# Attention stage of a gated cross-attention and MoE kernel: values projected for four pairs of heads, reciprocals from two activations and one Newton step, row norms two at a time, routing steps at other places, and the products with the values right behind the scores

## The chip, the cores and the metric

One core of a Trainium2 chip runs the whole program. The metric is the device time of one execution in microseconds (us). Only one core runs, so there is no other core to wait for.

## What is computed

The reference, cut to what matters (batch 8, 512 rows of x, 1024 rows of context, width 256, 16 heads of 64):

```python
lat, ctx = layer_norm(layernorm(x)), layer_norm(context)
q = lat @ Wq                       # 16 heads of 64
k, v = split(ctx @ Wkv)            # 16 heads of 64 each
k = apply_rope(k, cos, sin)        # cos and sin by token
attn = clip(q @ k.T * 64 ** -0.5, -11, 11)
out = softmax(attn) @ v
x = x + tanh(g_xattn) * (out @ Wo + bo)
# then, on layernorm(x): 64 experts, the best 8 of each row out of the
# best 4 of 8 groups (sigmoid scores plus a correction bias), and a shared expert
x = x + tanh(g_ffn) * (routed + shared)
```

## The kernel before

The program has four blocks in a row: `setup` (splits the weights into a high and a low part, so that TensorE multiplies them with the precision of fp32 in three passes), `attention`, `finish_routing`, `experts`. The change is in `attention` and in a few lines of `setup`.

**Pairs and steps.** `attention` works on 8 batches of 8 pairs of heads. A pair g goes through eight steps, c = 0 to 7. In step c of pair g TensorE does, in the order of the code of `step` for `pe`:

- the scores of token tile c of the *previous* pair (L897, six matmuls of 512 columns, written to the PSUM tile `scores`),
- where there is one, a tile of value projections (L913, `ps_v`), a half of the keys (L928, `ps_k`, in c = 0 and 4) or the queries (L940, `ps_k`, in c = 2) of the pair g itself,
- the products of values with exponentials (L952, written to `ps_o`) of the tile that was scored two steps earlier; the tile of the last two steps is done in c = 0 and 1 of the next pair, where also the sum of the exponentials over tokens is formed (L960, `ps_y`, c = 1),
- a half of the output projection (L989, `ps_y`) in c = 4 and 6.

A tile's exponentials go from ScalarE (L1029, `e`) to GpSimd, which clips them (L1124), and from there both to TensorE (L952) and to VectorE, which adds them up (L1297, `e_sum`). ScalarE also copies `ps_o` to `o_raw` in c = 2 (L1024); the product of tile 0 in c = 2 writes `ps_o` again and so waits for that copy (`s_oraw`). VectorE takes the reciprocals of the sums straight from `ps_y` in two halves of 256 columns (L1265, c = 2 and 3), and GpSimd multiplies `o_raw` with them (L1120, L1127).

Keys are turned by the rotary tables: ScalarE swaps quarters of `ps_k` into `k_sw` (L1043), VectorE multiplies with cosine and sine (L1281, L1282), GpSimd adds (L1116), ScalarE keeps the high part (L1051) and VectorE the low part (L1287). The low part of the queries is L1276 (`q_t`, semaphore `s_qlo`), for which the second half of the keys (c = 4) waits, since it writes `ps_k` again.

**Values.** `ps_v` holds 256 columns, two pairs of heads at once ("doubles"). Eight tiles of tokens make 32 groups of six matmuls in a batch. In batch 0 and in the first pair of every batch they stand in all eight steps of the even pairs; else four of them stand in each pair (`value_tile`). The last pair has none.

**Between batches** `boundary` turns the normalised rows `x_nat` of the next batch (L876, 24 transposes), which wait for the last normalised row tile (`norms.normed`) and for the last exponentials. Rows are normalised one tile of 128 rows at a time during the pairs (`prepare`): statistics on VectorE (L77, L82), the inverse root on GpSimd (L102; two operations for a context tile, seven for a latent tile), then L90 on VectorE. The last of them stands in c = 7 of the last pair.

**Routing.** From batch 1 on, the rows of the batch before are routed to experts between these steps (`route`, on VectorE, with short work of TensorE and ScalarE), and GpSimd sends the rows of the batch before that out by indirect DMA (L1105), one in each of the steps 0, 1, 4, 5, 7 of the pairs p = 1 to 6. Batches 2 to 7 are one loop body.

Every engine runs its own list in the order written; only semaphores connect them.

## Time and profile before

| | us |
|---|---|
| median of 3 runs | 2636.36 (2633.79 to 2646.41) |
| profiled execution, time | 2636.81 |
| profiled execution, span | 2634.7 |

| engine | busy us | share of the span |
|---|---|---|
| TensorE | 2331.4 | 88% |
| VectorE | 2171.2 | 82% |
| GpSimd | 1789.0 | 68% |
| ScalarE | 1420.3 | 54% |

TensorE runs at 2.4 GHz nearly everywhere (mean granted clock 0.959). These are averages over the whole program. What a change in the attention stage is worth is read from that stage: from the windows of single pairs, and from what TensorE waited for in them.

### The profile page before, as it was taken

The numbers are of one execution on the slowest core, as the hardware profiler recorded it, in microseconds if no ns is written. First come the engines' busy times: TensorE is split into PE (matmuls) and PEld (weight loads), VectorE is DVE, ScalarE is ACT, GpSimd is POOL, SyncE is SP. The second block draws the span as 40 slices with busy tenths as digits, with TensorE's granted clock in tenths as the row PEclk, the third lists the DMA queues.
The fourth block names the chain that finished last, engine by engine and source line by source line (L and its number), as shares of the span: only waits on it lengthen the run. The fifth ranks groups of instructions, "written<-read, shape, count | busy, mean of one in ns | idle before, by whom it ended". The sixth has DMA issues, their size and how long they took to land. (4 is left out here: it accounts for less than half of the span.)

```text
span 2634.7 us, 43493 instructions
## 1 busy us (share of the span) xinstructions
PE 2331.4 (88%) x12227; PEld 1360.2 (52%) x12227; DVE 2171.2 (82%) x3638; ACT 1420.3 (54%) x2520; POOL 1789.0 (68%) x1723
## 2 busy tenths in 40 slices
PE   2999999899989998998999899989987968999980
PEld 2554545454444544454545445444543646987870
DVE  4888788898888898898888898988897676688884
ACT  3666556565555555555665556555552323666660
POOL 3777676488858876886787588758874730077776
PEclk9999999899999999999999899999997988999995
DMA  8434334011102111120111112111114408799994
GB/s 298 155 124 159 112 112 162 29 58 55 63 29 78 57 51 44 57 69 31 65 53 54 40 57 77 53 42 55 56 49 147 157 16 291 235 329 322 332 322 138
DMA packets 166488, 305.11 MB, mean 116 GB/s; under 512 B 20914, under 2 KB 100210, under 8 KB 166002
## 3 DMA queue, kind: packets, MB, share of 16 engines
q1 hardware_dynamic: 138162, 234.88, 26.2%
q0 software_dynamic: 24576, 67.14, 7.7%
q8 instruction: 114, 1.87, 0.3%
q14 instruction: 116, 0.95, 0.1%
q10 hardware_dynamic: 3520, 0.27, 0.1%
HBM read 172.46 MB, written 129.76 MB: 115 GB/s over the span
## 5 line engine op out<-in xcount | busy, mean ns | idle before, releaser
L1124 POOL TENSOR_SCALAR e<-e 128x1024 f32<-128x1024 f32 x520 | 639.8, 1230 | 406.1 <-ACT e L1029 379.5
L1029 ACT ACTIVATE e<-scores 128x1024 f32<-128x1024 f32 x520 | 533.4, 1026 | 530.5 <-PE scores L897 509.0
L1297 DVE TENSOR_TENSOR e_sum<-e_sum,e 128x1024 f32<-128x1024 f32 x391 | 585.9, 1498 | 47.5 <-POOL e L1124 44.9
L952 PE MATMUL ps_o<-e,v 128*64 128x512 f32 x2088 | 567.7, 622 | 1.6 <-POOL e L1124 1.6
L897 PE MATMUL scores<-q_t,k_t 64*128 64x512 f32 x3120 | 505.3, 429 | 15.5 <-DVE affine L1242 14.2
L897 PEld LDWEIGHTS scores<-q_t,k_t 64*128 64x128 f32 x3120 | 255.0, 186 | 377.1 <-issue 255.4
L1831 POOL DMA_INDIRECT more<-results_in_blocks,index x256 | 245.4, 959 | 210.2 <-DMA results_in_blocks<-more 129.6
L1043 ACT ACTIVATE k_sw<-ps_k 32x512 f32<-32x512 f32 x512 | 301.3, 588 | 114.6 <-PE ps_k L928 110.0
L1105 POOL DMA_INDIRECT rows_in_blocks<-room,a_r_index_now x192 | 247.9, 1291 | 50.9 <-issue 50.1
L913 PE MATMUL ps_v<-wv,ctx_t 128*128 128x256 f32 x1536 | 252.5, 301 | 0.0
L928 PE MATMUL ps_k<-ctx_t,wqk 128*128 128x512 f32 x768 | 218.6, 422 | 33.8 <-DVE q_t L1276 33.5
L913 PEld LDWEIGHTS ps_v<-wv,ctx_t 128*128 128x128 f32 x1536 | 199.8, 190 | 94.2 <-issue 93.9
L1265 DVE RECIPROCAL r_den<-ps_y 128x256 f32<-128x256 f32 x132 | 230.4, 1746 | 13.6 <-PE ps_y L960 12.6
L1768 PE MATMUL ps_out<-down_all,room 128*128 (+1 forms) x640 | 194.5, 386 | 4.3 <-DVE room L1810 3.4
L928 PEld LDWEIGHTS ps_k<-ctx_t,wqk 128*128 128x128 f32 x768 | 140.3, 196 | 98.1 <-DVE q_t L1276 49.4
L1287 DVE TENSOR_TENSOR k_t<-k_c,k_t 128x512 fp32r<-128x512 f32 x128 | 118.5, 926 | 81.0 <-ACT k_t L1051 81.0
L952 PEld LDWEIGHTS ps_o<-e,v 128*64 128x64 f32 x2088 | 104.2, 136 | 143.1 <-issue 103.4
L1116 POOL TENSOR_TENSOR k_c<-k_c,k_sw 128x512 f32<-128x512 f32 x128 | 173.5, 1355 | 3.0 <-DVE k_sw L1282 1.3
L1793 DVE SCALAR_TENSOR_TENSOR x<-more,gate,x 128x256 f32<-128x256 f32 x256 | 123.2, 481 | 53.9 <-DMA more<-results_in_blocks,index 52.7
L1775 PE MATMUL ps_x<-ident,x_nat 128*128 128x128 f32 x640 | 125.5, 279 | 44.3 <-PEq L1312 27.6
L1731 ACT ACTIVATE x_nat<-ps_x 128x256 f32<-128x256 f32 x320 | 121.0, 378 | 78.2 <-PE ps_x L1775 75.0
L1748 PE MATMUL ps_hid<-x_nat,room 128*128 128x128 f32 x1024 | 157.7, 277 | 2.3 <-DVE room L1806 1.4
(287 smaller groups left out, 3606.3 us busy)
## 6 DMA issues: line engine op xcount, KB each, us to landing
rows_in_blocks<-room SPq DMA_DIRECT2D x16, 2560.0 KB, 9.8
x_nat<-rows_in_blocks SPq DMA_DIRECT2D x160, 256.0 KB
results_in_blocks<-more SPq DMA_DIRECT2D x80, 512.0 KB
wqk<-wqk_pairs SPq DMA_DIRECT2D x65, 512.0 KB, 3.5
wv<-wv_doubles SPq DMA_DIRECT2D x33, 512.0 KB, 3.3
wo<-in_L_xattn_Wo SPq DMA_DIRECT2D x66, 128.0 KB, 3.4
x_nat<-in_ctx SPq DMA_DIRECT2D x64, 128.0 KB, 3.2
down_all<-in_L_ffn_down_w SPq DMA_DIRECT2D x16, 512.0 KB, 8.6
```

What stands on the lines that cost most here:

```text
L897: mm = pe.matmul(scores[:, c % 2, hh * N:(hh + 1) * N], k_t[rows, att, kp, c * P:(c + 1) * P], q_t[rows, att, qp, :], start=(part == 0), s ...
L913: mm = pe.matmul(ps_v[:, 0:2 * P], ctx_t[:, a, cc, tile * P:(tile + 1) * P], wv[:, bb, cc], start=(k == 0), stop=(k == 5))
L928: mm = pe.matmul(ps_k[:], wqk[:, jj, bb, cc, 1], ctx_t[:, a, cc, half * N:(half + 1) * N], start=(k == 0), stop=(k == 5))
L952: mm = pe.matmul(ps_o[hh * DH:(hh + 1) * DH, :], v[:, tile, buf, hh * DH:(hh + 1) * DH], e[:, tile % 4, hh * N:(hh + 1) * N], start=(tile ...
L1029: act.activation(e[:, c % 4], scores[:, c % 2], ACT.Exp, scale=SCALE).then_inc(s_exp, 1)
L1043: st = act.activation(k_sw[to], ps_k[of], ACT.Copy)
L1105: pool.indirect_dma_start(xs_dram, bass.IndirectOffsetOnAxis(ap=router.index_now[:, t, k:k + 1], axis=0), router.rows[:, t], None).then_in ...
L1124: pool.tensor_scalar(e[:, c % 4], e[:, c % 4], EXP_HI, EXP_LO, ALU.min, ALU.max).then_inc(s_clip, 1)
L1265: dve.reciprocal(r_den[:, half], y_flat[:, half]).then_inc(s_rec, 1)
L1297: dve.tensor_tensor(total, e[:, 0] if c == 2 else total, e[:, tile % 4], ALU.add).then_inc(s_sum, 1)
L1768: pe.matmul(ps_y[:, i % 4, 0:D], act_g[:, i % 4], w, start=True, stop=True).then_inc(s_dn, 1)
L1831: pool.indirect_dma_start(land[:, k], None, y_dram[0:(E_R + (b + 1) * BODY) * P, :], bass.IndirectOffsetOnAxis(ap=at, axis=0)).then_inc(y_ ...
```

## The change

1. **Values of four pairs.** `DOUBLES` becomes `QUADS`: `ps_v` is used with 512 columns, `v` holds four pairs instead of three, and a batch has 16 groups of six matmuls. They stand in the first two of every four pairs (m = 0: c = 3, 5, 6, 7; m = 1: c = 1, 3, 5, 7), none in m = 2 and 3.
2. **Reciprocals.** In c = 2 ScalarE takes `Ln` and then `Exp` with scale -1 of the sums; in c = 3 VectorE makes one Newton step of it (a product of 512 columns, then one instruction over two SBUF tiles). The sign is put right by `minus_gate`. GpSimd's first half of `o_n` moves behind the clip of c = 3. Table sets are loaded by hand: `Tanh` of the router needs another one and back, once in a batch.
3. **Norms.** From batch 1 on two row tiles are normalised together, in the pairs 1 to 6 (statistics in c = 0, roots in c = 1, results in c = 6), and the context of a batch is loaded in one DMA.
4. **Routing steps** move: `number_blocks`, `place` and `cross` from the last pair to the first pair of the next batch, the steps of the groups to earlier places, and `e_sum` has one buffer instead of two. The first copies of rows go out one step later.
5. **Order.** The products of values with exponentials stand right behind the scores, ahead of the projections.

The core of the diff:

```diff
+                if attend or c < 2:
+                    tile = (c + 6) % 8
+                    buf = (m + 3 if c >= 2 else m + 2) % 4
+                    pe.wait_ge(s_clip, 1 + g * 8 + c)
+                    if c == 2:
+                        pe.wait_ge(s_oraw, g + 1)
+                    if m == 2 and c == 1:
+                        pe.wait_ge(s_v, 1 + (g // 4 + 1) * 8)
+                    for hh in range(2):
+                        mm = pe.matmul(ps_o[...], v[:, tile, buf, ...], e[:, tile % 4, ...], ...)
+                    mm.then_inc(s_pv, 1)
+
                 if first and c in (0, 4):
                     pe.wait_ge(t_lo, 1 + b * 6 + (2 if c == 0 else 4))
...
-                            mm = pe.matmul(ps_v[:, 0:2 * P], ctx_t[:, a, cc, tile * P:(tile + 1) * P], wv[:, bb, cc],
+                            mm = pe.matmul(ps_v[:], ctx_t[:, a, cc, tile * P:(tile + 1) * P], wv[:, bb, cc],
                                            start=(k == 0), stop=(k == 5))
...
-                if attend or c < 2:
-                    tile = (c + 6) % 8
-                    buf = values_of(m + 3 if c >= 2 else m + 2)
-                    pe.wait_ge(s_clip, 1 + g * 8 + c)
...
+                if c == 2:
+                    act.wait_ge(s_den, 1 + g + 1)
+                    act.activation(r_den[:], y_flat, ACT.Ln).then_inc(s_log, 1)
+                    act.wait_ge(s_log, g + 1)
+                    act.activation(r_den[:], r_den[:], ACT.Exp, scale=-1.0).then_inc(s_seed, 1)
...
-                if c in (2, 3):
-                    half = slice((c - 2) * D, (c - 1) * D)
-                    dve.wait_ge(s_den, 1 + g + 1)
-                    dve.reciprocal(r_den[:, half], y_flat[:, half]).then_inc(s_rec, 1)
...
+                if c == 3:
+                    dve.wait_ge(s_seed, g + 1)
+                    dve.tensor_tensor(o_n[:], y_flat, r_den[:], ALU.mult).then_inc(s_part, 1)
+                    dve.wait_ge(s_part, g + 1)
+                    dve.scalar_tensor_tensor(out=r_den[:], in0=o_n[:], scalar=2.0, in1=r_den[:],
+                                             op0=ALU.subtract, op1=ALU.mult).then_inc(s_rec, 1)
```

TensorE, steps 2 to 4 of pair 2 of the loop body, before (L897 scores, L940 queries, L952 products with the values, L913 values, L928 keys):

```order
L897 MATMUL scores<-q_t,k_t 128x512 [waits s_exp]
L897 MATMUL scores<-q_t,k_t 128x512 x5
L940 MATMUL ps_k<-lat_t,wqk 128x512 [waits s_cos]
L940 MATMUL ps_k<-lat_t,wqk 128x512 x5
L952 MATMUL ps_o<-e,v 64x512 [waits s_oraw,s_clip]
L952 MATMUL ps_o<-e,v 64x512
...
L928 MATMUL ps_k<-ctx_t,wqk 128x512 [waits s_cos,s_qlo]
L928 MATMUL ps_k<-ctx_t,wqk 128x512 x5
L952 MATMUL ps_o<-e,v 64x512 [waits s_clip]
L952 MATMUL ps_o<-e,v 64x512
```

The same place after (L908 scores, L921 products with the values, L964 queries, L952 keys):

```order
L908 MATMUL scores<-q_t,k_t 128x512 [waits s_exp]
L908 MATMUL scores<-q_t,k_t 128x512 x5
L921 MATMUL ps_o<-e,v 64x512 [waits s_oraw,s_clip]
L921 MATMUL ps_o<-e,v 64x512
L964 MATMUL ps_k<-lat_t,wqk 128x512 [waits s_cos]
L964 MATMUL ps_k<-lat_t,wqk 128x512 x5
...
L921 MATMUL ps_o<-e,v 64x512 [waits s_clip]
L921 MATMUL ps_o<-e,v 64x512
L952 MATMUL ps_k<-ctx_t,wqk 128x512 [waits s_cos,s_qlo]
L952 MATMUL ps_k<-ctx_t,wqk 128x512 x5
```

The product of tile 0, which waits for `o_raw`, has passed ahead of the queries, and the product of tile 2 ahead of the second half of the keys; the value tile that stood between them is gone from this pair.

VectorE, between the sine product of c = 1 and the sum of c = 3, pair 3 of the loop body, before:

```order
L1282 TENSOR_TENSOR k_sw<-k_sw,sin_t 128x512
...
L1265 RECIPROCAL r_den<-ps_y 128x256 [waits s_den]
...
L1297 TENSOR_TENSOR e_sum<-e 128x1024 [waits s_den,s_clip]
L1265 RECIPROCAL r_den<-ps_y 128x256 [waits s_den]
L1276 TENSOR_TENSOR q_t<-ps_k,q_t 128x512 [waits s_qe]
```

After:

```order
L1321 TENSOR_TENSOR k_sw<-k_sw,sin_t 128x512
...
L1336 TENSOR_TENSOR e_sum<-e 128x1024 [waits s_den]
L1308 TENSOR_TENSOR q_t<-ps_k,q_t 128x512 [waits s_qe]
L1311 TENSOR_TENSOR o_n<-ps_y,r_den 128x512 [waits s_seed]
L1313 SCALAR_TENSOR_TENSOR r_den<-o_n,r_den 128x512 [waits s_part]
```

The two reciprocals ahead of the low part of the queries (`q_t`) are gone, and two instructions stand behind it.

## Rows read from the trace of the kernel before

**Rows 1.** The page, part 1: engine, busy us, share of the span, count.

```profile
PE 2331.4 (88%) x12227; PEld 1360.2 (52%) x12227; DVE 2171.2 (82%) x3638; ACT 1420.3 (54%) x2520; POOL 1789.0 (68%) x1723
```

**Rows 2.** Windows: length, busy of PE, PEld, DVE, ACT, POOL, clock.

```profile
65.21:250.84 185.63, 185.63 (x952) 94.29 (x950) 157.46 (x167) 113.40 (x171) 138.81 (x126) 1.00 0.42 141
997.72:1240.01 242.29, 225.03 (x1136) 117.32 (x1137) 213.06 (x293) 138.51 (x208) 185.69 (x174) 0.98 0.16 54
1212.59:1240.01 27.42, 17.81 (x86) 7.70 (x83) 26.52 (x38) 11.35 (x15) 16.08 (x14) 0.97 0.06 19
1240.01:1255.62 15.61, 13.82 (x62) 9.91 (x64) 9.12 (x16) 10.91 (x18) 1.84 (x2) 0.72 0.14 51
```

**Rows 3.** Waits of PE from 60 to 1990 us: us in total, times, longest.

```profile
PE scores L876 <- DVE x_nat L90: 42.5, 7, 6.6
PE ps_k L928 <- DVE q_t L1276: 33.5, 20, 3.1
PE ps_y L313 <- DVE x L1272: 13.7, 7, 2.1
PE ps_y L437 <- DVE x L1272: 9.4, 7, 1.4
```

**Rows 4.** Groups by line: count, busy us, mean ns, idle before.

```profile
L1265 DVE RECIPROCAL r_den<-ps_y 128x256 f32<-128x256 f32 x132 | 230.4, 1746 | 13.6 <-PE ps_y L960 12.6
L1281 DVE TENSOR_TENSOR k_c<-ps_k,cos_t 128x512 f32<-128x512 f32 x128 | 87.7, 685 | 29.9 <-ACT k_sw L1043 29.1
L1287 DVE TENSOR_TENSOR k_t<-k_c,k_t 128x512 fp32r<-128x512 f32 x128 | 118.5, 926 | 81.0 <-ACT k_t L1051 81.0
```

**Rows 5.** Timeline of PE, start and length in us, steps 0 to 2 of a pair.

```profile
1063.46 1.65 PE L928 MATMUL ps_k<-ctx_t,wqk 128*128 128x512 f32 x6
1065.04 1.08 PE L952 MATMUL ps_o<-e,v 128*64 128x512 f32 x4
1066.05 0.96 PE L897 MATMUL scores<-q_t,k_t 64*128 64x512 f32 x6
1066.94 0.98 PE L913 MATMUL ps_v<-wv,ctx_t 128*128 128x256 f32 x6
1067.85 1.08 PE L952 MATMUL ps_o<-e,v 128*64 128x512 f32 x4
1068.76 1.03 PE L960 MATMUL ps_y<-e_sum,ones_dh 128*64 128x512 f32 x4
1069.72 0.97 PE L897 MATMUL scores<-q_t,k_t 64*128 64x512 f32 x6
...
1078.75 1.08 PE L952 MATMUL ps_o<-e,v 128*64 128x512 f32 x4
```

**Rows 6.** Timeline of ACT at the same steps.

```profile
1065.15 2.39 ACT L1043 ACTIVATE k_sw<-ps_k 32x512 f32<-32x512 f32 x4 [0.47 <-PE ps_k L928]
1067.56 1.02 ACT L1029 ACTIVATE e<-scores 128x1024 f32<-128x1024 f32 x1
...
1069.06 0.60 ACT L1024 ACTIVATE o_raw<-ps_o 128x512 f32<-128x512 f32 x1 [0.19 <-PE ps_o L952]
```

**Rows 7.** Timeline of POOL from step 1 of the same pair on.

```profile
1068.79 1.03 POOL L1124 TENSOR_SCALAR e<-e 128x1024 f32<-128x1024 f32 x1 [0.72 <-ACT e L1029]
...
1076.25 1.04 POOL L1124 TENSOR_SCALAR e<-e 128x1024 f32<-128x1024 f32 x1
...
1077.65 1.88 POOL L297 TENSOR_TENSOR a_r_rstd<-a_r_rstd,minus_half 128x4 f32<-128x4 f32 x1
...
1085.47 1.03 POOL L1124 TENSOR_SCALAR e<-e 128x1024 f32<-128x1024 f32 x1
...
1091.64 1.04 POOL L1124 TENSOR_SCALAR e<-e 128x1024 f32<-128x1024 f32 x1
```

**Rows 8.** Timeline of PE at the boundary in front of batch 2.

```profile
511.86 4.31 PE L876 MATMUL scores<-ident,x_nat 128*128 128x128 f32 x24 [5.49 <-DVE x_nat L90]
518.71 1.65 PE L897 MATMUL scores<-q_t,k_t 64*128 64x512 f32 x6 [2.54 <-DVE affine L1242]
```

More of the change, by code:

```diff
@@ L15 @@
 PAIRS = H // 2
[L16 removed]
+QUADS = PAIRS // 4
 NT = N // P
@@ L629, in _ @@
             act.wait_ge(wq_loaded, 16 * 4)
-            for n in range(3 * DOUBLES):
+            for n in range(5 * QUADS):
                 for c in range(C2):
@@ L670, in _ @@
         def _(dve):
-            for n in range(3 * DOUBLES):
+            for n in range(5 * QUADS):
                 dve.wait_ge(w_hi, C2 * (n + 1))
@@ L1097, in prepare @@
                                       n_step + (1 - jj) * norms.LAT_STEPS)
-            places = [(0, 7)] + [(p, c) for p in range(1, 7) for c in (0, 1, 4, 5, 7)] + [(7, 0)]
+            places = [(p, c) for p in range(1, 7) for c in (0, 1, 4, 5, 7)] + [(7, 0), (7, 1)]
             places.sort()
@@ L1167, in finish_slots @@
                 if part == 0:
-                    router.r, router.k = r, crossing[0]
+                    router.r, router.k = r, numbered[0]
+                    router.number_blocks(dve, range(3, 6))
+                elif part == 1:
+                    router.place(dve)
+                    router.cross(dve)
+                elif part == 2:
                     router.slots(dve)
-                elif part == 1:
+                elif part == 3:
                     router.order_slots(dve)
```

210 lines of the change are left out of this document (115 added, 95 removed).

## The prediction

> **What bounds the kernel now.** The page comes first: TensorE is busy for 88% of the span and VectorE for 82% [rows 1]. That is an average, so I went to windows inside the attention stage. In batch 0 TensorE is busy for all 185.63 us of the window, with VectorE at 85%, so nothing but TensorE's own work sets the time there. A later batch lasts 242.29 us, of which TensorE works 225.03. The missing 17 us lie at few places: the last pair (27.42 us with 17.81 of work) and the boundary behind it (15.61 us, at a granted clock of 0.72) [rows 2]. The waits of TensorE name the reasons, all of them VectorE: the last normalised row tile, 42.5 us in 7 boundaries; the low part of the queries in front of the second half of the keys, 33.5 us; and the rows `x` that VectorE adds up late, 13.7 and 9.4 us, in front of router work [rows 3]. In short, TensorE's work is the bound, with VectorE late at the end of each batch. The other rows show what a step costs (rows 5) and what ScalarE and GpSimd do meanwhile (rows 6, 7).
>
> **What the change takes away, per batch of 1 to 7.**
>
> Values. A group of six matmuls of 256 columns costs 0.91 us from start to start (1066.94 to 1067.85), six of 512 columns for the keys cost 1.58 (1063.46 to 1065.04) [rows 5]. 32 x 0.91 = 29.1 becomes 16 x 1.58 = 25.3: -3.8, and -3.5 since some of the old groups stand in front of keys or queries and cost a little less there. Bound above: 512 columns cost twice 0.91, nothing gained. I take the keys' row, which is the same shape.
>
> The boundary. The last norm goes to pair 6, and about 7 us of VectorE's work leave the last pair. The 42.5 / 7 = 6.1 us wait [rows 3] goes; what is late next is the exponential of tile 7 (1.02 us [rows 6], with a product of 1.01 to cover it), 0.25 us. That is -5.8. Behind it the first score started 6.85 us after the first transpose [rows 8], and the product of sums 15.61 us after it in the window at clock 0.72 [rows 2]. Without the long idle time before it I expect 6.4 and then, at full clock, 0.89 + 1.01 + 1.58 + 0.89 + 0.91 = 5.3, together 11.7. Of the 3.9 us between, 1.6 are two value groups that only move: -2.3.
>
> The low part of the queries. VectorE's two reciprocals of 1746 ns [rows 4] stood in front of it and are gone. The wait was 33.5 / 7 = 4.8: -4.8. In place of 3.5 us a pair VectorE has two instructions of 512 columns: the first reads PSUM and SBUF, as `k_c` does (685 ns), the second two SBUF tiles, as `k_t` (926 ns) [rows 4], together 1.6. They stand behind the queries' low part, so only the output product in c = 4 waits for them.
>
> Router waits. 13.7 + 9.4 us in 7 batches = 3.3 [rows 3], both from a late VectorE: -3.3, at worst half of it.
>
> Together -3.5 - 5.8 - 2.3 - 4.8 - 3.3 = **-19.7 us**.
>
> **What it adds.** This comes mostly from the new order, since TensorE executes its list in order and now meets each product before the projection that used to cover its wait.
>
> `o_raw` in c = 2. After the keys' matmuls start, ScalarE runs `k_sw` (start +1.69, 2.39 us), an exponential (+4.10, the next start 0.92 later) and the copy of `o_raw` (0.60): ready at +5.67 [rows 6]. TensorE reaches the product after 1.58 + 0.89 + 0.91 + 0.96 + 0.89 = 5.24 [rows 5]. Before, 1.6 us of queries stood between; now it waits 0.43. In pair m = 1 a value group is in between and hides it: 6 of 8 pairs, +2.6. Bounds 0 and 6 x 0.8.
>
> The clip of tile 2, in front of the product in c = 4. GpSimd starts the clip of tile 1 at 1068.79 and that of tile 2 at 1076.25, 7.46 us later: in between stand a row transfer, seven root operations and the sum of the keys. With two root operations (c = 5 and 6 of the pair) the same stretch takes 6.17, from 1085.47 to 1091.64 [rows 7]. TensorE's product waited for nothing at 1078.75, because queries, a value group and the keys covered it [rows 5]. In a pair without value groups (p = 2, 3, 6, 7) TensorE now wants it 1.90 + 5.24 + 0.43 + 1.01 + 1.59 + 0.89 + 1.01 + 0.89 = 12.96 us after the pair begins, and tile 1's clip starts at 1.90 + 4.10 + 1.02 = 7.02. In pair 2 (seven operations) the clip is ready at 7.02 + 7.46 + 1.04 = 15.52: +2.5. In pairs 3 and 6 (two) at 14.23: +1.25 each. Pair 7 has none, and pairs 0, 1, 4, 5 have a value group, 1.58, in front. Sum +5.0. Bounds: 2 if GpSimd is quicker because VectorE disturbs it less, 10 if it is late from pair to pair.
>
> The first output product in c = 4. In pair 2 GpSimd also has the router's root (1.88 us [rows 7]) ahead of it: +1.65. In pairs 0 and 5 the moved routing steps (some 5 and 3 us of VectorE in c = 1 and 2) push the Newton step: +0.7 and +0.8. Sum +3.2, bounds 1 and 6.
>
> The rest (products in c = 0, the sums' product in c = 1 when VectorE is behind after pair 0): +1.0, bounds 0 and 3. Together **+11.8**. The new `Ln` and `Exp`, 0.6 us each as `o_raw` [rows 6], lie in ScalarE's idle time, and their chain behind the queries' copy (0.6 + 0.6 + 0.6 + 1.6) ends before GpSimd gets to `o_n`; without that cover they would add about 1 us a pair. ScalarE works 138.51 of 242.29 us [rows 2].
>
> Net per batch -7.9, times 7 = **-55.3**. Batch 0 had no wait to lose: values -1.6 (12 of its old groups stood in front of keys or queries), `o_raw` +2.6, the clip of tile 2 twice 1.1 (no row transfers yet): **+3.2**. A third more of `v` is cleared at the start, +1, for which I have no row. The one big context load replaces eight small ones at a DMA share of 0.16 [rows 2] and is needed two pairs later: nothing. Sum -51. The profiled execution took 2636.8 us and the median of the runs is 2636.4, so both give 2586.
>
> **Two rules of the skill that speak against it.** The row shows one thing for VectorE: 512 elements cost 685 ns with one operand in PSUM and 926 ns with both in SBUF [rows 4]. The Trainium skill (SBUF — State Buffer, "SBUF: two separate sides") says that a VectorE instruction with two SBUF inputs locks GpSimd's reads out for its whole length. The old reciprocal read PSUM only, so by that rule the second Newton instruction is new trouble for GpSimd; it is rival 3 below. The profile's rows show `Exp` and `Copy` in steady alternation with no gap for tables [rows 6]. The Trainium skill (ScalarE: Activation LUTs, "What ACT_TABLE_LOAD costs") gives 2.66 us for a switch of table sets; two in each of seven batches would be 37 us of ScalarE by that page, an estimate, and 2623 if TensorE waited for all of it. ScalarE's idle time says it does not.
>
> **Rivals.**
> 1. *The waits fall together.* One wait of TensorE lets ScalarE and GpSimd catch up, so that `o_raw`, clip and output product are paid once. Half of 11.8: -13.8 a batch, 2544. For it: no product waited for a clip in before's batches. Against it: `o_raw` comes first in the pair and delays its own chain.
> 2. *Values at twice the old price*: +3.5 x 8, 2614. Against it stands the keys' row.
> 3. *GpSimd held up by the second Newton instruction*: 0.93 in six pairs a batch, 5.6: net -2.3 x 7, batch 0 +7: 2629.
> 4. *Slower: GpSimd late in every pair.* The order takes the cover from all pairs, not from three. If all four pairs without values lose pair 2's 4.6 us and the others 1.6, that is 24.8 + 1 against 19.7: +6.1 x 7 + 8 + 1, 2689. It decides from 2.7 us of new waits a pair; I count 1.5. For it: GpSimd works 185.69 of 242.29 us, and a pair without values is only 23 us of TensorE, in which GpSimd needs 23 to 25 by its rows. Against it: fewer root operations (22 instead of 44 a batch).
>
> **How the numbers follow.** Forecast 0.50 at 2586 (its own range 2560 to 2612); rival 1 0.21; rival 2 0.06; rival 3 0.14; rival 4 0.09. From 2540 to 2640 leaves out some of rival 1 and all of rival 4. A measurement of this kernel can tell about 0.5% from no change, 2623 to 2650. Faster: forecast, rivals 1 and 2, a little of 3: 0.77. Within: most of 3: 0.14. Slower: 0.09.
>
> **What would show it.** Right: no wait of `scores` for `x_nat`, none or little of `ps_k` for `q_t`; new rows of waits of `ps_o` for `o_raw` (about 20 us in all) and for clips of `e` (about 40), of `ps_y` for `o_n` (20); a value group of 1.58; batches of about 235 us, with the gain at the boundary and a loss in pairs 2, 3 and 6. Wrong: waits for clips also in pairs with values, or GpSimd busy over 90% in the window of a batch (rival 4); no new wait above 5 us (rival 1); clip durations longer behind the Newton step (rival 3).

## The result, and the profile after

| | before, us | after, us |
|---|---|---|
| median | 2638.38 (4 runs) | 2661.60 (2659.68 to 2663.80, 4 runs) |
| profiled execution, span | 2634.7 | 2657.9 |
| start of the last product of sums (`ps_y`, end of the attention stage) | 1999.2 | 2021.7 |
| length of batch 0 | 223.7 | 231.5 |
| length of batches 1 to 6, mean | 243.0 | 244.3 |
| start of the first batch | 49.7 | 51.0 |
| last batch, to its product of sums | 267.7 | 273.5 |

The ratio is 1.0083 [1.0059, 1.0106]: **slower** by 0.8%, which is clear of the noise, where 2586 us (2540 to 2640) had been forecast. Of the difference of 23 us, 22.5 stand before the last product of sums; what follows it takes some 636 us in both. Batches are taken here from the first transpose to the next batch's, and the last one ends with that product of sums. Before's row of the page is in [rows 1]; this is after's (engine, busy us, share, count):

```profile
PE 2310.5 (87%) x11459; PEld 1286.0 (48%) x11459; DVE 2116.3 (80%) x3593; ACT 1498.1 (56%) x2536; POOL 1804.5 (68%) x1569
```

TensorE and VectorE have less to do, and the program takes longer. The windows that answer to [rows 2] follow: the stretch in batch 0, batch 4, its last pair, the boundary behind it up to the product of sums, and pair 2 of batch 4 (length, busy PE, PEld, DVE, ACT, POOL, clock).

```profile
65.21:250.84 185.63, 178.20 (x822) 84.63 (x820) 137.54 (x160) 114.53 (x162) 135.30 (x122) 1.00 0.41 141
1010.77:1256.54 245.77, 223.62 (x1040) 108.77 (x1041) 207.12 (x288) 147.86 (x211) 186.66 (x153) 0.97 0.16 53
1235.27:1256.54 21.27, 18.01 (x84) 7.79 (x85) 20.43 (x24) 12.65 (x18) 15.12 (x12) 1.00 0.09 34
1256.54:1272.01 15.47, 10.76 (x50) 6.29 (x52) 10.57 (x14) 8.78 (x14) 3.38 (x3) 0.78 0.05 15
1087.60:1119.68 32.08, 26.37 (x116) 12.05 (x112) 27.04 (x41) 18.15 (x27) 27.37 (x27) 0.89 0.17 60
```

In the stretch of batch 0 TensorE was busy for all 185.63 us before and is busy for 178.20 now: it has room that the other engines don't fill. The last pair is 6.1 us shorter (27.42 before), the boundary only 0.1 us (15.61). All other pairs together are 9.8 us longer. TensorE's waits, as in [rows 3], from 60 to 1990 us:

```profile
PE ps_o L921 <- POOL e L1147: 56.2, 31, 3.7
PE ps_y L1001 <- POOL o_n L1151: 22.9, 24, 3.0
PE scores L887 <- DVE affine L1278: 18.5, 6, 3.3
PE ps_o L921 <- ACT o_raw L1038: 18.5, 35, 1.4
PE scores L908 <- ACT affine L1020: 12.4, 7, 2.3
PE ps_y L973 <- DVE e_sum L1336: 10.0, 7, 1.5
PE ps_k L952 <- DVE q_t L1308: 9.1, 6, 1.5
PE scores L887 <- DVE x_nat L90: 4.5, 1, 4.5
```

The waits of [rows 3] for `x_nat` (42.5), `q_t` (33.5) and `x` are gone or small. In their place stand waits for clips and `o_n` of GpSimd, for `o_raw`, and at the boundary for `affine`. Three groups that answer to [rows 4] and [rows 5] (count, busy us, mean ns): the values and the two instructions of the Newton step.

```profile
L937 PE MATMUL ps_v<-wv,ctx_t 128*128 128x512 f32 x768 | 212.1, 411 | 0.0
L1313 DVE SCALAR_TENSOR_TENSOR r_den<-o_n,r_den 128x512 f32<-128x512 f32 x64 | 50.4, 788 | 2.2
L1311 DVE TENSOR_TENSOR o_n<-ps_y,r_den 128x512 f32<-128x512 f32 x64 | 44.0, 687 | 16.9 <-ACT r_den L1064 16.9
```

### The profile page after: what moved, and what is told of

It is laid out like the page before. It is cut to its first block and busy times, and to the rows that moved or that the text cites. A ratio compares the mean times of both kernels' runs of the same rounds, so it can differ in the third digit from the quotient of the medians.

```text
span 2657.9 us, 41338 instructions
## 1 busy us (share of the span) xinstructions
PE 2310.5 (87%) x11459; PEld 1286.0 (48%) x11459; DVE 2116.3 (80%) x3593; ACT 1498.1 (56%) x2536; POOL 1804.5 (68%) x1569
## 5 line engine op out<-in xcount | busy, mean ns | idle before, releaser
L1147 POOL TENSOR_SCALAR e<-e 128x1024 f32<-128x1024 f32 x520 | 673.8, 1296 | 405.0 <-ACT e L1043 345.8
L1336 DVE TENSOR_TENSOR e_sum<-e_sum,e 128x1024 f32<-128x1024 f32 x391 | 628.9, 1608 | 92.0 <-POOL e L1147 86.9
L921 PE MATMUL ps_o<-e,v 128*64 128x512 f32 x2088 | 575.4, 629 | 76.9 <-POOL e L1147 57.3
L908 PE MATMUL scores<-q_t,k_t 64*128 64x512 f32 x3120 | 507.8, 430 | 14.2 <-ACT affine L1020 12.4
L908 PEld LDWEIGHTS scores<-q_t,k_t 64*128 64x128 f32 x3120 | 255.9, 187 | 276.8 <-issue 246.9
L1132 POOL DMA_INDIRECT rows_in_blocks<-room,a_r_index_now x192 | 272.2, 1418 | 49.0 <-issue 44.2
L921 PEld LDWEIGHTS ps_o<-e,v 128*64 128x64 f32 x2088 | 105.8, 136 | 275.4 <-issue 162.6
L952 PE MATMUL ps_k<-ctx_t,wqk 128*128 128x512 f32 x768 | 220.1, 423 | 9.1 <-DVE q_t L1308 9.1
L937 PE MATMUL ps_v<-wv,ctx_t 128*128 128x512 f32 x768 | 212.1, 411 | 0.0
L952 PEld LDWEIGHTS ps_k<-ctx_t,wqk 128*128 128x128 f32 x768 | 139.4, 195 | 148.0 <-issue 103.6
L1143 POOL TENSOR_TENSOR k_c<-k_c,k_sw 128x512 f32<-128x512 f32 x128 | 191.4, 1496 | 14.5 <-DVE k_sw L1321 11.8
L937 PEld LDWEIGHTS ps_v<-wv,ctx_t 128*128 128x128 f32 x768 | 134.2, 188 | 126.6 <-issue 103.9
L1001 PE MATMUL ps_y<-wo,o_n 128*128 128x256 f32 x528 | 150.4, 409 | 31.3 <-POOL o_n L1151 28.4
L1814 PE MATMUL ps_x<-ident,x_nat 128*128 128x128 f32 x640 | 125.3, 278 | 47.6 <-PEq L1351 27.6
```

The costliest lines, as they stand in the source:

```text
L908: mm = pe.matmul(scores[:, c % 2, hh * N:(hh + 1) * N], k_t[rows, att, kp, c * P:(c + 1) * P], q_t[rows, att, qp, :], start=(part == 0), s ...
L921: mm = pe.matmul(ps_o[hh * DH:(hh + 1) * DH, :], v[:, tile, buf, hh * DH:(hh + 1) * DH], e[:, tile % 4, hh * N:(hh + 1) * N], start=(tile ...
L937: mm = pe.matmul(ps_v[:], ctx_t[:, a, cc, tile * P:(tile + 1) * P], wv[:, bb, cc], start=(k == 0), stop=(k == 5))
L952: mm = pe.matmul(ps_k[:], wqk[:, jj, bb, cc, 1], ctx_t[:, a, cc, half * N:(half + 1) * N], start=(k == 0), stop=(k == 5))
L1132: pool.indirect_dma_start(xs_dram, bass.IndirectOffsetOnAxis(ap=router.index_now[:, t, k:k + 1], axis=0), router.rows[:, t], None).then_in ...
L1147: pool.tensor_scalar(e[:, c % 4], e[:, c % 4], EXP_HI, EXP_LO, ALU.min, ALU.max).then_inc(s_clip, 1)
```

## The experiments

Each group of runs shares a chip with runs of before. In all groups but one (e6 to e9) the stages behind the attention take some 140 us longer than in the tables above, so times are compared only as ratios within a group, or in the traces up to the last product of sums, whose start is called **the end** here. It repeats well: 2021.7 and 2024.1 for the kernel after, 1981.8 and 1979.9 for the best variant, on two chips each. All runs but e2, e14 and e17 have the one buffer of `e_sum`, also where part 4 isn't named.

| run | parts | ratio to before | end, us | end less 1999.2 (before, first chip) |
|---|---|---|---|---|
| after | 1 to 5 | 1.0083 [1.0059, 1.0106] | 2021.7 | +22.5 |
| e18_after_again | 1 to 5 | 1.0080 [1.0061, 1.0099] | 2024.1 | +24.9 |
| e1_order_back | 1 to 4 | 0.9933 [0.9906, 0.9959] | 1983.8 | -15.4 |
| e2_order_alone | 5 | 1.0127 [1.0097, 1.0156] | 2031.2 | +32.0 |
| e3_behind_2_and_4 | 1 to 4, 5 but in steps 2 and 4 | 1.0152 [1.0129, 1.0175] | 2041.3 | +42.1 |
| e5_filler | 1 to 5, filler in pair 2 | 1.0077 [1.0051, 1.0102] | 2026.8 | +27.6 |
| e6_doubles | 2, 3, 4 | 0.9944 [0.9927, 0.9960] | 1991.9 | -7.3 |
| e7_reciprocals | 1, 3, 4 | 1.0236 [1.0219, 1.0253] | 2062.6 | +63.4 |
| e8_both | 3, 4 | 1.0154 [1.0137, 1.0171] | 2042.5 | +43.3 |
| e9_back_roots_later | 1 to 4, roots in step 4 | 0.9971 [0.9959, 0.9983] | 1992.8 | -6.4 |
| e10_part3_alone | 3 | 0.9943 [0.9922, 0.9963] | 1987.7 | -11.5 |
| e11_transfers | 1 to 4, no transfers in pair 2 | 0.9933 [0.9910, 0.9957] | 1984.7 | -14.5 |
| e12_all_but_step_0 | 1 to 4, 5 but in step 0 | 0.9932 [0.9909, 0.9955] | 1981.8 | -17.4 |
| e19_step_0_again | the same | 0.9922 [0.9903, 0.9942] | 1979.9 | -19.3 |
| e13_routing_back | 1, 2, 3 | 1.0013 [1.0002, 1.0024] | 2005.9 | +6.7 |
| e14_step_0_alone | 5 in step 0 only | 1.0130 [1.0101, 1.0159] | 2049.2 | +50.0 |
| e17_before_all_but_0 | 5 but in step 0 | 0.9963 [0.9947, 0.9980] | 2009.1 | +9.9 |
| e15_keys_first | 1 to 4, keys ahead of scores | 0.9978 [0.9965, 0.9991] | 2005.2 | +6.0 |
| e16_blocks_later | as e12, block counts later | 0.9933 [0.9912, 0.9954] | 2000.4 | +1.2 |

For e14 to e17, which share one chip, the last column and the ratio don't fit: the ratios say +36, -10, -6 and -19 us of before's 2802.04, so the column is 12 to 20 us higher, where in all other groups the two agree within 8 us. Before itself took 17 to 29 us longer on this chip than in the other groups with the long later stages (2773.05, 2784.26 and 2785.51). No trace of before from this chip was kept, so whether its attention stage is longer there is open. These four are compared by their ratios or with each other.

### Which part costs: the order

In `step` for `pe` of the kernel after, the block of the products goes back behind the projections:

```diff
-                if attend or c < 2:            # behind the scores
-                    ... products with the values ...
                 ... values, keys, queries ...
+                if attend or c < 2:
+                    ... products with the values ...
                 if c == 1:
                     pe.wait_ge(s_add, 2 + g * 2)
```

> The changed kernel with part 5 undone: the products of values with exponentials stand behind the projections again, parts 1 to 4 stay. Theory A (the new order takes the cover from TensorE's waits, and the idle time costs a lower clock behind it): the waits of ps_o for e (57 us) and for o_raw (18 us) fall to under 10 us together, pair 2 of a batch goes from 32.1 to about 26 us and runs at full clock, pairs 3 and 6 lose 1 to 2 us; 8 to 10 us less per batch, so 2575 to 2595 us, faster than the kernel before by 2%. Rival B (the other four parts cost the time: GpSimd and VectorE are as late whatever TensorE's order): the waits only move from ps_o to ps_k and ps_y, batches stay at 244 to 246 us, 2645 to 2665 us.

> The kernel before with part 5 alone. Theory A: o_raw is waited for in the pairs without a value tile in step 1, and the clips only in the last pair, since a value group of 0.9 us stands in most steps: +1 to +4 us per batch, 2645 to 2670 us. Rival B (the order costs nothing by itself): 2630 to 2642 us. Rival C (the order alone costs what the whole change lost and more): 2690 us or more.

> The changed kernel with the products behind the projections in the steps 2 and 4 alone, ahead of them in all others. Theory A says that only these two places cost (o_raw in step 2, the clip of tile 2 in step 4): as fast as with the whole order undone within 0.3%, 2575 to 2600 us. If the places in steps 0 and 1 (keys half, sums) count too, it stays 10 us or more behind the kernel with the whole order undone.

The second is before with part 5 alone, the third has the block at both places, behind the projections `if c in (2, 4)`. Measured: the order costs 38 us of after's attention stage and 32 us of before's; without it the kernel is 0.7% faster than before. So part 5 is the loss. But neither forecast of e1 came out: the waits for clips fell to 6.9 us, as theory A had it, and those for `o_n` rose to 46.4, as rival B had it, and pair 2 stays at 30.7 us. And undoing the order in steps 2 and 4, where the prediction had its waits, made the kernel 20 us slower still (waits for `o_n` 58.2 us, for `q_t` 24.9): that step of the argument fell here. It also shows that the places don't simply add up; why the steps 2 and 4 alone cost so much was not followed.

### Is it the clock in pair 2?

In after's pair 2 the clock falls to 0.89 behind a wait of 3.7 us for a clip. The filler keeps TensorE at work there; its 14 matmuls compute nothing that is used.

```diff
+                    if p == 2 and c == 4:
+                        for _ in range(14):
+                            pe.matmul(ps_v[:], ctx_t[:, 0, 0, 0:P], ctx_t[:, 0, 0, 0:N], start=True, stop=True)
                     pe.wait_ge(s_clip, 1 + g * 8 + c)
```

> The changed kernel with 14 idle matmuls of 512 columns (3.8 us at full clock) into a free PSUM tile in step 4 of pair 2 of each batch from 1 on, in front of the wait for the clip. Theory A1 (TensorE's clock falls during the wait of 3.7 us and the 8 us behind it run slower): keys in this step take 1.65 instead of 2.93 us, pair 2 gets 2 to 3 us shorter, 14 to 20 us in all, 2642 to 2650 us. Rival (the clock is not the cost; GpSimd is late and sets the end of the pair anyway): pair 2 stays at 32 us, 2655 to 2668 us.

Pair 2 of batch 4, the columns as above:

```profile
1090.32:1122.42 32.10, 27.47 (x130) 13.11 (x126) 27.03 (x41) 18.17 (x27) 27.66 (x27) 1.00 0.17 59
```

The clock is 1.00 all through the pair, and it takes 32.10 us instead of 32.08. The slow clock was real and cost this pair nothing; with full clock TensorE only waits more.

### What parts 1 to 4 are worth

e6, e7 and e8 have the products behind the projections, as before and e1 have them. e6 takes the values of two pairs at a time as before, e7 the reciprocals:

```diff
-                if c == 3:
-                    dve.wait_ge(s_seed, g + 1)
-                    dve.tensor_tensor(o_n[:], y_flat, r_den[:], ALU.mult).then_inc(s_part, 1)
-                    ...
+                if c in (2, 3):
+                    half = slice((c - 2) * D, (c - 1) * D)
+                    dve.wait_ge(s_den, 1 + g + 1)
+                    dve.reciprocal(r_den[:, half], y_flat[:, half]).then_inc(s_rec, 1)
```

> The kernel after with the products behind the projections again (part 5 undone) and with the values of two pairs at a time as before (part 1 undone): parts 2 to 4 alone. Reference: the same with four pairs at a time took 0.9933 of before. Theory A (values of four pairs put all of TensorE's value work into two of every four pairs, and the pairs without it run at the pace of GpSimd, so the work that is saved there isn't time that is saved): TensorE has 3.7 us more work per batch and 3 to 5 us fewer waits; ratio between 0.988 and 0.995, waits of ps_y for o_n in pairs 2, 3, 6 and 7 at most half of 46 us. Rival B (the values' 3.7 us are worth their price wherever they lie): 8 x 3.7 = +29 us, ratio 1.004.

> The kernel after with part 5 undone and part 2 undone (VectorE takes the reciprocals straight from ps_y, GpSimd's first half of o_n stands ahead of the clip of step 3): parts 1, 3 and 4 alone. Theory C (the Newton step makes r_den late and disturbs GpSimd): the mean of o_n's first half goes from 1.5 us back to about 0.9, clips from 1.30 to about 1.24, waits of ps_y for o_n from 46 us to under 15; the waits of ps_k for q_t return with 20 to 30 us; net 0 to -20 us against the kernel with parts 1 to 4, ratio 0.986 to 0.993. Rival D (taking the reciprocals from VectorE is worth the 4.8 us a batch of the prediction): +25 us and more, ratio 1.003 or above.

> The kernel after with parts 1, 2 and 5 undone: the norms in groups of two and the moved routing steps (parts 3 and 4) alone. These take the wait of 42.5 us for the last normalised row tile away and cost TensorE nothing. If theories A and C hold, this is the fastest of the four: ratio 0.980 to 0.988. If B and D hold, it is worse than parts 1 to 4 together: above 0.9933, about 1.00.

e6 came out as theory A's ratio, though its waits for `o_n` fell to 32.5 us only, from 46.4. By ratio it can't be told from e1 (0.9944 and 0.9933); in the traces e1's end is 8.1 us earlier. Theory C fell and rival D held: with the reciprocals back on VectorE the end is 78.9 us later (50.6 without part 1). The waits for `o_n` did fall, from 46.4 to 3.1 us (60 to 1990 us), but those for `q_t` rose from 12.1 to 86.3. e8 was the surprise: the norms in groups and the moved routing steps, which I had taken for pure gain, cost 43 us by themselves. TensorE's longest waits in e8, from 60 us to the end, and its last pair in batch 4, first on TensorE, then on VectorE (start, length):

```profile
PE ps_k L941 <- DVE q_t L1308: 84.4, 22, 6.6
PE scores L889 <- DVE affine L1274: 17.2, 6, 3.2
```

```profile
1245.42 0.97 PE L910 MATMUL scores<-q_t,k_t 64*128 64x512 f32 x6
1253.02 2.93 PE L941 MATMUL ps_k<-ctx_t,wqk 128*128 128x512 f32 x6 [6.62 <-DVE q_t L1308]
```

```profile
1241.68 3.43 DVE L464 SCALAR_TENSOR_TENSOR a_r_opened<-a_r_over,a_r_opened 128x64 f32<-128x64 f32 x3
1245.03 1.75 DVE L1297 RECIPROCAL r_den<-ps_y 128x256 f32<-128x256 f32 x1
1246.70 1.16 DVE L1330 TENSOR_TENSOR e_sum<-e 128x1024 f32<-128x1024 f32 x1
1247.78 2.97 DVE L471 TENSOR_TENSOR a_r_opened<-a_r_opened 128x64 f32<-128x64 f32 x3
1250.67 1.74 DVE L1297 RECIPROCAL r_den<-ps_y 128x256 f32<-128x256 f32 x1
1252.34 0.62 DVE L1308 TENSOR_TENSOR q_t<-ps_k,q_t 128x512 fp32r<-128x512 f32 x1
```

The counting of blocks (L464) stands in step 1 and their numbering (L471) in step 2, each ahead of a reciprocal and both ahead of `q_t`, for which TensorE waits. In before both stood ahead of the first reciprocal, and L471 took 0.75 us there, not 2.97. Was it the routing steps or the norms? e10 is e8 with before's places of the routing steps and of the first row copies, e13 is e1 with them:

```diff
-                if (p, c) == (7, 1):
-                    router.overflow(dve)
-                    router.count_blocks(dve)
-                if (p, c) == (7, 2):
-                    router.number_blocks(dve, range(0, 3))
+                if (p, c) == (7, 0):
+                    router.overflow(dve)
+                if (p, c) == (7, 1):
+                    router.count_blocks(dve)
+                    router.number_blocks(dve, range(0, 3))
+                if (p, c) == (7, 4):
+                    ... number_blocks(3 to 5), then place, cross, and the groups' steps in pairs 5 and 6 ...
```

> The kernel after with parts 1, 2 and 5 undone and the routing steps and first row copies at before's places: of the five parts only the norms in groups of two are left (with the single buffer of e_sum). Parts 3 and 4 together took 1.0154 of before, with 84.4 us of waits of ps_k for q_t, the longest 6.6 us in the last pair. If the moved routing steps are the cause (they stand on VectorE ahead of the reciprocals and so of q_t in pairs 5 and 7), q_t falls to 25 to 40 us, the last pair gets its gain and the ratio is 0.985 to 0.996. If the grouped norms are the cause, the ratio stays at 1.008 or above.

> The kernel after with part 5 undone and the routing steps and first row copies at before's places: parts 1, 2 and 3. Against 0.9933 with part 4. Since no reciprocals stand on VectorE any more, the moved steps delay q_t in the last pair alone (12 us in all): without them these waits go, but 6 us of VectorE's work return into the last pair behind step 3 and make the boundary's affine later (wait now 18 us): ratio 0.991 to 0.997. If part 4 costs here what it costs beside the reciprocals, the ratio is below 0.985.

The routing steps: moved beside the reciprocals they cost 54.8 us of the attention stage (e10 to e8), moved without the reciprocals they bring 22.1 (e13 to e1), so e13's ratio of 1.0013 lies outside its forecast: with before's places the transposes wait 34.8 us for `affine`, not 17.9. Part 3 alone is 0.6% faster than before. Its waits show how the boundary's gain shrinks:

```profile
PE ps_k L940 <- DVE q_t L1315: 38.5, 27, 3.3
PE scores L888 <- DVE affine L1281: 29.0, 6, 5.5
```

`x_nat` no longer holds the transposes, but the same late VectorE reaches `affine` late, 29.0 us where before had 12.1.

### Does GpSimd set pair 2?

Pair 2 is long in e1 too (30.7 us, where TensorE works 26.7 and GpSimd 26.3). e9 moves GpSimd's root operations from step 1 to step 4, e11 takes all five row transfers out of pair 2:

```diff
-                    if 1 <= p <= GROUPS_OF_ROWS and c == 1:
+                    if 1 <= p <= GROUPS_OF_ROWS and c == 4:
```

```diff
+            each = {1: (0, 1, 4, 5, 7), 3: (0, 1, 4, 5, 7), 4: range(8), 5: (0, 1, 4, 5, 7), 6: (0, 1, 4, 5, 7), 7: range(4)}
+            places = [(p, c) for p in each for c in each[p]]
```

> The kernel after with part 5 undone, and the root operations of two row tiles on GpSimd (seven operations in pairs 1 and 2, two in pairs 3 to 6) in step 4 of a pair instead of step 1. If GpSimd's queue ahead of the clips of steps 1 and 2 sets the pace of pair 2 (31 us against 25 to 28 in pairs 1 and 3), pair 2 loses 2 to 4 us and the ratio falls from 0.9933 to 0.985 to 0.990. If it is GpSimd's whole work in that pair (27 of 31 us), wherever it stands, the ratio stays within 0.002 of 0.9933.

> The kernel after with part 5 undone (0.9933 of before) and with the five row transfers of pair 2 moved: three to steps 2, 3 and 6 of pair 4, two to steps 2 and 3 of the last pair. Pair 2 is the one in which GpSimd works 26.3 of 30.7 us while TensorE works 26.7. If GpSimd's whole work sets that pair, five transfers of 1.4 us less make it 26 to 27.5 us, and pair 4, which TensorE fills, stays at 33: ratio 0.982 to 0.987. If VectorE (25.4 us) or the chain of latencies sets it, it loses less than 1 us a batch: 0.991 to 0.994.

Pair 2 of batch 4, in e9 and then in e11:

```profile
1072.01:1102.33 30.32, 24.15 (x115) 10.60 (x115) 27.23 (x41) 17.38 (x25) 27.50 (x27) 1.00 0.15 50
```

```profile
1070.06:1099.71 29.65, 26.25 (x117) 11.61 (x115) 25.88 (x40) 16.75 (x24) 22.73 (x22) 0.88 0.08 27
```

Neither helps; e9 is 0.4% slower than e1, which its forecast had not named. GpSimd's work falls from 26.3 to 22.7 us in e11 and the pair by 1.0 us, which pair 4 loses again (34.7 against 33.3). e9 turned the waits for `o_n` (46.4 us in e1, 19.6 now) into waits for `e_sum` (14.6, now 47.7; all from 60 to 2000 us). GpSimd's amount of work does not set this pair; what does is left open.

### Where in the pair the order costs

> The kernel after with the products with the values behind the keys again in step 0 alone, ahead of the projections in all other steps. With the products behind in steps 2 and 4 alone it was slower (1.0152), with all behind faster (0.9933), after itself 1.0083. If the cost of the order comes from step 0, where the first half of the keys, and with it the whole chain over k_sw, the queries, r_den and o_n, starts one product later in every pair, the ratio is 0.993 to 0.998. If it comes from the waits for o_raw and the clips in steps 2 and 4, as the prediction has it, the ratio stays at 1.006 to 1.009.

> The kernel before with the product with the values ahead of the projections in step 0 alone. The whole of part 5 on the kernel before gave 1.0127, +32 us in the attention stage. If step 0 carries the cost (keys, k_sw and all behind them one product of 1.01 us later, in every pair), the ratio is 1.008 to 1.014. If the cost in before comes from the waits for q_t, o_raw and clips in steps 2 to 7, it is 0.998 to 1.003.

> The kernel before with the products with the values ahead of the projections in all steps but step 0. If step 0 carries the cost of the order, the ratio is 0.998 to 1.003; the waits for o_raw and clips appear (15 us and 10 to 20 us), and those of ps_k for q_t fall by about as much. If the other steps carry it, 1.008 to 1.013.

```diff
-                if attend or c < 2:            # behind the scores
+                if (attend or c < 2) and c != 0:
                     ... products with the values ...
                 ... values, keys, queries ...
+                if (attend or c < 2) and not c != 0:
+                    ... products with the values ...
```

With the old order **in step 0 alone** the whole loss of part 5 is gone (-40 us at the end against after). On the kernel before, step 0 alone costs as much as the whole part (1.0130 and 1.0127), and all other steps together nothing (0.9963). e14 and e17, on one and the same chip, differ by 43 us in time and 40 at the end. Run side by side on one chip in five rounds:

> The kernel after, unchanged, timed beside the next one on one chip. If its loss is its own and not the chip's, the ratio to before is 1.006 to 1.011 again, and the last product of sums of the attention stage starts at 2020 to 2024 us.

> The kernel after with the old order in step 0 alone. If step 0 is worth what the single runs showed (40 us of the attention stage), the ratio to before is 0.992 to 0.996, 1.3 to 1.6% under the kernel after beside it. If the difference between the chips made it, the two are within 0.5% of each other.

After took 2808.91 us, the variant 2764.85, before 2785.51. **The kernel after with the old order in step 0 beats both**: 0.8% under before, 1.6% under after.

The loss is spread over a batch. Pair by pair, from one product of sums to the next, e12 is shorter than after by 1.1, 0.0, 1.5, 0.3, -0.2, 1.5, 1.0 and 0.7 us (means of batches 2 to 6). Pair 5 of batch 4 shows how one product does it. In after the keys of step 0 (L952) stand behind the product (L921). TensorE, ScalarE, GpSimd and VectorE in turn, start and length:

```profile
1172.35 1.08 PE L921 MATMUL ps_o<-e,v 128*64 128x512 f32 x4
1173.36 1.65 PE L952 MATMUL ps_k<-ctx_t,wqk 128*128 128x512 f32 x6
...
1178.43 1.08 PE L973 MATMUL ps_y<-e_sum,ones_dh 128*64 128x512 f32 x4
...
1191.04 1.13 PE L1001 MATMUL ps_y<-wo,o_n 128*128 128x256 f32 x4 [1.06 <-POOL o_n L1151]
```

```profile
1175.05 2.39 ACT L1055 ACTIVATE k_sw<-ps_k 32x512 f32<-32x512 f32 x4 [1.46 <-PE ps_k L952]
```

```profile
1178.69 1.03 POOL L1147 TENSOR_SCALAR e<-e 128x1024 f32<-128x1024 f32 x1 [1.31 <-ACT e L1043]
...
1185.89 1.18 POOL L1147 TENSOR_SCALAR e<-e 128x1024 f32<-128x1024 f32 x1 [0.45 <-ACT e L1043]
```

```profile
1178.82 1.45 DVE L1321 TENSOR_TENSOR k_sw<-k_sw,sin_t 128x512 f32<-128x512 f32 x1
...
1186.20 1.14 DVE L395 TENSOR_TENSOR a_r_cmp_b<-a_r_cmp_b,room 128x256 f32<-128x256 f32 x1
1187.26 0.68 DVE L1308 TENSOR_TENSOR q_t<-ps_k,q_t 128x512 fp32r<-128x512 f32 x1
```

The same instructions in e12, where the product (L978) stands behind the keys:

```profile
1152.52 1.67 PE L952 MATMUL ps_k<-ctx_t,wqk 128*128 128x512 f32 x6
1154.12 1.08 PE L978 MATMUL ps_o<-e,v 128*64 128x512 f32 x4
...
1158.62 1.08 PE L986 MATMUL ps_y<-e_sum,ones_dh 128*64 128x512 f32 x4
...
1170.00 1.02 PE L1014 MATMUL ps_y<-wo,o_n 128*128 128x256 f32 x4
```

```profile
1154.22 2.40 ACT L1068 ACTIVATE k_sw<-ps_k 32x512 f32<-32x512 f32 x4 [0.46 <-PE ps_k L952]
```

```profile
1157.87 1.03 POOL L1160 TENSOR_SCALAR e<-e 128x1024 f32<-128x1024 f32 x1 [0.32 <-ACT e L1056]
```

```profile
1158.98 0.68 DVE L1334 TENSOR_TENSOR k_sw<-k_sw,sin_t 128x512 f32<-128x512 f32 x1
...
1165.59 0.42 DVE L395 TENSOR_TENSOR a_r_cmp_b<-a_r_cmp_b,room 128x256 f32<-128x256 f32 x1
1165.93 0.68 DVE L1321 TENSOR_TENSOR q_t<-ps_k,q_t 128x512 fp32r<-128x512 f32 x1
```

Count from the product of sums (1178.43 and 1158.62). ScalarE's copies end 0.99 us before it instead of 2.00, one product later. So the exponential behind them and its clip start one product later too: +0.26 instead of -0.75. VectorE itself is not late: it reaches the product with the sine at +0.39 instead of +0.36. But now the clip is running, and that instruction takes 1.45 us instead of 0.68. A second such meeting follows, of a routing step (L395, 1.14 us instead of 0.42) with the clip at 1185.89. The two together put `q_t` at +8.83 instead of +7.31: 1.0 us of one engine has become 1.5 us of another. The Newton step and `o_n` follow it, and TensorE's output product, at +11.38 without a wait, now starts at +12.61 after a wait of 1.06.

This pair loses the same 1.5 us in batches 3 and 5 (1.4 in the latter). The other pairs lose theirs in other ways: in pair 0 of batch 4 the sine product itself starts 1.05 us later and `q_t` with it, in pair 2 the clips are 1.0 and then 1.5 us later, and pair 1 loses nothing. The meetings with GpSimd are not more frequent in after as a whole: the sine product takes 774 ns there in the mean and 781 in e12, and VectorE's busy time differs by 6 us in the whole program. What differs is where they fall. That step 0 carries the loss is shown by the runs; the chain is shown for pair 5 and only sketched for the others.

> The kernel after with part 5 undone and, in the pairs 1 to 7 of a batch, the first half of the keys ahead of the scores of step 0, with ScalarE's four k_sw copies ahead of the exponential of step 0. Theory (the start of the keys sets the pace of the pairs that TensorE does not fill): k_sw is ready 1 us earlier, pairs 2, 3, 6 and the last lose 0.5 to 1 us each, 2 to 4 us a batch, ratio 0.982 to 0.989. Rival (the keys may start late, but not at the price of the exponential of step 0, which is now 2.4 us later and with it a clip and e_sum): ratio at 0.993 or above, with new waits of ps_o for e and of ps_y for e_sum.

> The kernel after with the old order in step 0 alone (0.9932) and with overflow, count_blocks and number_blocks(0 to 2) of the last pair in steps 4 and 5 instead of 1 and 2. If they delay the last pair by standing ahead of q_t and the Newton step, q_t's wait (0.9 us a batch) and o_n's in the last pair (up to 3.6 us) go: -1 to -3 us a batch, ratio 0.985 to 0.990. If VectorE's whole work in the last pair is the limit (20.4 of 20.7 us), the time comes back as a longer wait of the transposes for affine (now 18 us): ratio 0.992 to 0.996.

e15 puts the first half of the keys ahead of the scores (and ScalarE's copies ahead of the exponential), e16 counts the blocks in steps 4 and 5 of the last pair:

```diff
+                if project and c == 0 and not first:
+                    ... keys, first half ...
                 if attend:
                     ... scores ...
```

```diff
-                if (p, c) == (7, 1):
+                if (p, c) == (7, 4):
                     router.overflow(dve)
                     router.count_blocks(dve)
-                if (p, c) == (7, 2):
+                if (p, c) == (7, 5):
```

e15 is behind e1, by 0.45% in the ratios (some 12 us): the waits for `o_n` rise from 46.4 to 63.5 us, and batches 1 to 6 take 242.5 us in the mean instead of 239.3. So "earlier keys are better" is not the rule; that what counts is where in the cycle the engines meet fits all these runs, but is argued. e16 brings nothing: its ratio is e12's (0.9933 and 0.9932, each with 0.2% of uncertainty). In the trace the wait for `q_t` goes, the pairs stay as long as in e12, and the transposes wait 29.5 us for `affine` instead of 18.2, as the rival had it.

## Why the prediction was wrong

Forecast per batch of 1 to 7: -19.7 of gains, +11.8 of new waits. Measured against before, over the whole attention stage: parts 1 to 4 -15.4 us (forecast some -138), part 5 +38 (all new waits, forecast some +87, of which some belonged to the other parts). The sum came out at +22.5 instead of -51. Two steps failed. The gains counted each removed wait of TensorE in full as time won, and only a ninth of it came. And the cost of the new order was put on what the moved products wait for; it comes from step 0, which the sum held at +1.0 a batch, and this is what turned a gain of 15 us into a loss.

- **Values.** Right in price: six matmuls of 512 columns cost 1.58 us and more, and start to start the values of batch 4 take 25.1 us instead of 28.8. Wrong as time: batches 1 to 7 got 2.2 us each in the mean (e6 to e1), batch 0 lost 4.6 us (224.8 to 229.5) where -1.6 stood, and the first batch starts 2.4 us later. "Batch 0 had no wait to lose" was true and the wrong question. The likely reason, not tested alone: TensorE's work had been spread evenly, 26.5 to 28.1 us in each of before's pairs of batch 4 but the last; now it works 30.7 us in pair 0 and 23.8 in pair 3, and two of every four pairs have no values to cover anything with. (The +1 for the longer start, for which the forecast had no row, is 1.3 from before to after.)
- **Boundary, -5.8 and -2.3.** The wait for `x_nat` went as said, and the last pair fell from 27.42 to 21.27. But "what is late next is the exponential" looked only at the engine in front. VectorE comes to `affine` only 4.3 us after the transposes begin, and holds the third block of them:

```profile
1256.54 1.96 PE L887 MATMUL scores<-ident,x_nat 128*128 128x128 f32 x16 [0.24 <-ACT e L1043]
1261.76 1.92 PE L887 MATMUL scores<-ident,x_nat 128*128 128x128 f32 x8 [3.26 <-DVE affine L1278]
1265.13 1.65 PE L908 MATMUL scores<-q_t,k_t 64*128 64x512 f32 x6 [1.45 <-ACT affine L1020]
```

```profile
1257.98 2.05 DVE L1336 TENSOR_TENSOR e_sum<-e_sum,e 128x1024 f32<-128x1024 f32 x1
1260.81 1.53 DVE L1278 TENSOR_SCALAR affine<-scores,gain,shift 128x512 f32<-128x512 f32 x2 [0.77 <-issue]
```

  Transposes to first score took 8.6 us instead of the 6.4 of the forecast (6.85 in [rows 8]), at clock 0.78 and not at full speed.
- **Router waits, -3.3.** These went as said, from 23.1 us to 3.1.
- **The low part of the queries, -4.8.** This wait did go, to 9.1 us in all. But the term stood beside the routing steps at "some 5 and 3 us of VectorE in c = 1 and 2", priced at 0.7 and 0.8. Alone with before's reciprocals they cost 54.8 us. Part 2 did not win 33.5 us of waits for nothing; it mostly paid for part 4, as e7, e8 and e10 show together. The price of the two new instructions was right, 687 and 788 ns for 1.6 us in all, but by chance: the 926 ns of `k_t` are a mean of 672 at the least and 1556 at the most, with and without GpSimd in the way, and not what two inputs in SBUF cost. The second instruction has a median of 693.
- **`o_raw`, +2.6 a batch.** Waits of 18.5 us, about the 20 named: the mechanism was right. **Clips, +5.0**: 56.2 us against 40, the longest in pair 2. **Output product, +3.2**: 22.9 against 20. So the signs named for "right" nearly all came, and yet prove nothing, for the waits for clips and `o_n` are there and cost nothing: e12 has 32.2 us of the one and 30.2 of the other and is as fast as e1, which meets its products behind the projections. This is rival 1 (the waits fall together), taken further than it was put. `o_raw` is different: in e12 its wait is 1.7 us, so it goes with step 0, behind which ScalarE's copies start a product later. It can't be the whole of it, since on the kernel before e14 has none of it and costs as much as e2, which has 15.5 us.
- **"The rest (products in c = 0 ...): +1.0, bounds 0 and 3."** This term is the step that made the sign wrong. Batch 4 takes 245.77 us in after and 239.93 in e12: **5.8 us a batch** (5.3 in the mean of batches 1 to 6, and 5.8 from e18 to e19 on one chip). I priced what the moved product waits for, in step 0 nearly nothing, and not what now waits behind it: the keys, and with them the chain of four engines.
- **Rival 4** (GpSimd late in every pair) had the sign, with a chance of 0.09, but not the cause. GpSimd is busy for 186.66 of 245.77 us, 76% and not over 90, and e11 took a seventh of its work out of pair 2 for nothing. **Rival 3** (chance 0.14) had a true part: clips went from 1230 to 1295 ns in the mean (31 of the 248 that took 1.2 us and more start beside the second Newton instruction), and the first half of `o_n` from 943 to 1527. The second is not the Newton step's doing in the way that the rival had it: `o_n` waits for that step to end, and then starts beside a sum (L1336) in 58 of 64 cases; in before it mostly started beside a reciprocal or beside nothing. Before, then after:

```profile
L1120 POOL TENSOR_TENSOR o_n<-o_raw,r_den x65: 714/732/1775, 72.2 to 1982.6; 128x256 f32<-128x256 f32 x65
```

```profile
L1151 POOL TENSOR_TENSOR o_n<-o_raw,r_den x64: 731/1592/1761, 73.8 to 1984.2; 128x256 f32<-128x256 f32 x64
```

  The columns are the shortest, the median and the longest in ns. The root operations (L102) fell from 203 to 104 us, and clips (+34 us for 520), the first half of `o_n` (+36), row transfers (+24) and the keys' sums (+18), all in the same number as before, ate it.

The sums were made wait by wait, each wait removed counted as time won. In this kernel TensorE, VectorE and GpSimd work 224, 207 and 187 of 246 us, and a removed wait came back under another name: e1 has some 80 us less of waits for `x_nat`, `q_t` and `x` than before, and 44 more for `o_n`, 17 for `affine` at the boundary, 8 for `e_sum` and 5 for clips (60 to 2000 us).

## What to carry to other kernels

- When an instruction is moved forward, price first what it is moved in front of, and follow that to the end of its chain on all engines; what the moved instruction itself waits for can be free. Here one product of 1.01 us in front of one projection in each pair cost 5 to 6 us a batch, and the same move at the seven other places together, with step 0 left alone, nothing.
- A removed wait is worth time only up to the next engine that is late in the same place; look for that engine before writing the gain down, and be wary of a sum in which every removed wait counts in full.
- Look twice before making work that covers others cheaper by making it larger and rarer: here it took the cover from half of the pairs, won 2.2 of 3.5 us a batch, and in the batch that TensorE had filled the saving turned into a loss of 4.6 us.

## What the runs showed of the hardware

- The same VectorE instruction takes 0.68 us or twice that, by what GpSimd does. The product with the sine (512 elements, both inputs in SBUF) ran in 674 ns at the least, 681 in the median and 1502 at the most; at 1178.82 it took 1.45 us beside a clip that had started 0.13 us earlier, at 1158.98 in e12 0.68, with the clip just over and a row transfer starting at 1159.17. It goes both ways, as the medians of the first half of `o_n` above show (732 in before, where it mostly starts beside a reciprocal that reads PSUM or beside nothing, 1592 in after, where it starts behind the start of a sum with both inputs in SBUF). The Trainium skill (SBUF — State Buffer, "SBUF: two separate sides") says that of a VectorE instruction with two SBUF inputs and a GpSimd one that reads SBUF, whichever starts first holds the shared port for its whole instruction, and the other waits; the trace agrees in both directions, but for starts that lie closer than 0.03 us: a sum recorded at 1182.13 took 2.40 us, and GpSimd's addition at 1182.16 its usual 1.28.
- Two loads of tables cost 2.57 us of ScalarE a batch: each of the 14 in the batches took 1283 ns, with 0.02 us or less of idle time on either side, as at 1165.59, where the activation starts behind a load from 1164.29. The Trainium skill (ScalarE: Activation LUTs, "What ACT_TABLE_LOAD costs") adds a drain of some 1380 ns to each, so two loads would take 5.3 us by that page, an estimate; no such gap stands in this trace.
- A granted clock of 0.89 in pair 2 cost the pair nothing (32.08 us and, at full clock, 32.10).
